# Mixture-of-experts stage: routed experts on their own tokens only, rows moved into expert order by indirect transfers

## The reference, cut to what matters

```python
logits = ((x @ wt.T) + repeat(g @ wg.T, s)) / 2        # 8 experts, g is per batch
scores = softmax(logits)
topk_w, topk_idx = top_k(scores, 2); topk_w /= topk_w.sum(-1) + 1e-20
gp = leaky(einsum('th,ehm->etm', x, w_gate)); up = einsum('th,ehm->etm', x, w_up)   # m = 128
y_all = einsum('etm,emh->eth', gp * up, w_down)
y = sum of the two chosen y_all, each by its weight
p = leaky(x @ sw_gate) * (x @ sw_up) @ sw_down         # shared expert, 256 wide
y = y + p
```

## Time and profile before

| what | us |
|---|---|
| median of 3 runs (lowest, highest) | 1475.9 (1474.04, 1478.81) |
| profiled execution: its time | 1475.61 |
| profiled execution: span, first to last instruction | 1473.6 |
| TensorE busy in the span | 1290.3 |
| VectorE busy | 1039.8 |
| ScalarE busy | 767.6 |
| GpSimd busy | 553.1 |
| next phase's first transfer is issued at | 440.37 |

### The profile page before, as it was taken

How to read it: one execution, slowest core, us unless ns; L and a number is a source line. 1 busy time by engine, 2 the same in 40 slices (tenths; PEclk the granted TensorE clock), 3 DMA queues, 4 the chain that set the end, 5 groups by cost and what they waited for, 6 DMA issues and landing times. The chain is left out here.

```text
span 1473.6 us, 30046 instructions
## 1 busy us (share of the span) xinstructions
PE 1290.3 (88%) x8705; PEld 996.1 (68%) x8710; DVE 1039.8 (71%) x2788; ACT 767.6 (52%) x1940; POOL 553.1 (38%) x834
## 2 busy tenths in 40 slices
PE   4989989998964799999999999999999999944866
PEld 2867877787842577777777777777777788731223
DVE  5566666656554777787877778868877877763986
ACT  3222223232221566666766766666767676624853
POOL 1333332333322675444444344444444444510004
PEclk9999999999986799999999999999999999976987
DMA  6232211220205300001000000010010000202115
GB/s 227 70 118 101 72 57 71 100 83 15 74 31 177 100 16 2 2 2 30 2 30 4 2 30 2 2 32 2 1 30 2 16 2 2 74 15 61 57 57 172
DMA packets 51043, 71.55 MB, mean 49 GB/s; under 512 B 4497, under 2 KB 43665, under 8 KB 48850
## 3 DMA queue, kind: packets, MB, share of 16 engines
q1 hardware_dynamic: 50338, 69.60, 14.3%
q10 hardware_dynamic: 560, 0.20, 0.1%
HBM read 57.07 MB, written 12.72 MB: 47 GB/s over the span
## 5 line engine op out<-in xcount | busy, mean ns | idle before, releaser
L837 POOL TENSOR_SCALAR scores<-scores,att_rinv 128x128 f32<-128x128 f32 (+3 forms) x512 | 264.3, 532 | 204.4 <-DVE att_rinv L1049 204.4
L893 ACT ACTIVATE scores<-scores,att_top 128x128 f32<-128x128 f32 (+3 forms) x512 | 281.5, 553 | 89.2 <-DVE att_top L1031 88.9
L1031 DVE CUSTOM_DVE_ANT_0 scores<-ps_y,w_bias_b,null_s 128x128 f32<-128x128 f32 x448 | 229.4, 547 | 100.5 <-PE ps_y L1181 89.1
L261 POOL TENSOR_TENSOR act_w<-act_g,wide_w 128x512 f32<-128x512 f32 x64 | 105.5, 1649 | 282.9 <-DVE act_g L379 277.4
L1192 PE MATMUL ps_up<-ident,scores 128*128 128x128 f32 x1280 | 191.7, 274 | 8.2 <-DVE keep L1059 6.2
L1180 PE MATMUL ps_y<-k_hh,q_hl 128*128 128x256 f32 (+2 forms) x512 | 187.6, 376 | 12.8 <-DVE att_top L1031 5.9
L1202 PE MATMUL ps_a<-keep,w_val 128*64 128x128 f32 x2560 | 197.2, 284 | 0.3 <-DVE keep L1059 0.3
L901 ACT ACTIVATE keep<-ps_up 128x128 f32<-128x128 f32 (+3 forms) x256 | 111.9, 437 | 156.1 <-PE ps_up L1192 153.2
L208 ACT ACTIVATE hid_hi<-hid 128x512 fp32r<-128x512 f32 x80 | 50.5, 631 | 241.8 <-DVE hid L397 241.7
L1192 PEld LDWEIGHTS ps_up<-ident,scores 128*128 128x128 f32 x1280 | 150.3, 140 | 30.9 <-issue 10.4
L844 POOL TENSOR_SCALAR w_q_hm<-q_hl 64x512 fp32r<-64x512 f32 x128 | 76.7, 612 | 239.0 <-ACT q_hl L916 239.0
(11 more groups left out here) (236 smaller groups left out, 2594.6 us busy)
## 6 DMA issues: line engine op xcount, KB each, us to landing
wide_w<-token_w_dram SPq DMA_DIRECT2D x16, 1024.0 KB, 4.7
x_raw<-in_x_t_dram SPq DMA_DIRECT2D x8, 512.0 KB, 3.7
x_nat<-in_x_nat_dram SPq DMA_DIRECT2D x8, 512.0 KB, 4.7
x_dram<-x_nat SPq DMA_DIRECT2D x8, 512.0 KB, 2.9
w_x1t<-x_dram SPq DMA_DIRECT2D x8, 512.0 KB, 4.0
c_dram<-out_raw SPq DMA_DIRECT2D x8, 512.0 KB, 3.2
c2t<-c_dram SPq DMA_DIRECT2D x8, 512.0 KB, 3.7
x_tile<-x_dram SPq DMA_DIRECT2D x8, 512.0 KB, 4.4
```

The source lines that it names most:

```text
L261: nc.gpsimd.tensor_tensor(act_w[:, k % 2], act_g[:, k % 2], wide_w[:, k], ALU.mult).then_inc(sem.act_w_ready, 1)
L837: nc.gpsimd.tensor_scalar(s, s, rinv[:, pp, q, hh:hh + 1], 0.0, ALU.mult, ALU.add).then_inc(sem.p_normed, 1)
L893: nc.scalar.activation(s, s, ACT.Exp, scale=-1.0, bias=top[:, pp, q, hh:hh + 1], accum_out=lsum[:, pp, q, hh:hh + 1]).then_inc(sem.exp_don ...
L1031: dve.tensor_tensor_reduce(scores_of(pp, hh, q), psS[:, hh, 0:n], bias_of(w, h)[:, CAUSAL[q]:CAUSAL[q] + n], 1.0, null_s[:, par, q, h:h + ...
```

## The change

The routed experts now work on the tokens that chose them. The batches are taken in two halves of 4 batches, 2048 tokens, 16 tiles of 128 tokens (HT = 16). In a half each token has two rows in a list in memory (`dram.xs`), ordered by expert, each expert's part filled up with rows of zeros to whole tiles of 128. The most tiles that can be needed is XT = 16 x 2 + 7 = 39, and the program always runs 39 a half, in JOBS = 20 steps of two tiles (the last has one); STEPS_X = 40.

The order of the work:

- Router: all of x is loaded first (`early_x`, 8 transfers of 512 KB). TensorE makes all logits as float32 products, tokens in the partitions, three for each of the 32 tiles of 128 tokens, the third of them adding the batch's condition.
- Routing, once for all tokens: VectorE finds both chosen experts (`pick`), TensorE counts with two products against a triangle and a matrix of ones (`ranks`, `counts`), VectorE works out each row's slot (`places_of`), the slots of the zero rows (`pads_of`) and each tile's expert (`owners_of`).
- GpSimd scatters x into `dram.xs`: one indirect transfer for each tile of tokens and choice, 32 a half, and 7 of zeros.
- The 16 shared units run as before, with their result copied to `p_all` by ScalarE. GpSimd's `weigh` is gone.
- Routed steps, pipelined over four stages: load two tiles (SyncE), transpose them, split hi and lo, gate and up with the tokens stationary and the expert's weights (256 columns, gate beside up) moving, leak, product, transpose, split, down, copy to `ys`, store to `dram.ys` (issued by ScalarE). TensorE reads each tile's expert into a register (`owner_of`) and uses it in the address of the weights.
- GpSimd gathers for each batch the 8 sets of 128 rows that its tokens need, and VectorE adds them to `p_all` with their weights (`combine`). The quantised product is as before, with its two casts on ScalarE (`widen`) in place of VectorE. Three batches do this beside routed steps (`DONE_AT`), the other five after them.

All of it is written out without loops. The mask of a head now waits for the bias of its pair of heads (`bias_in[h // 2]`).

```diff
-                def weigh(b, k):
-                    s = NE * b + k
-                    pool.wait_ge(sem.wide_in[2 * k // E], 16 * (b + 1))
-                    pool.wait_ge(sem.act_g_ready, s + 1)
-                    nc.gpsimd.tensor_tensor(act_w[:, k % 2], act_g[:, k % 2], wide_w[:, k], ALU.mult
-                                            ).then_inc(sem.act_w_ready, 1)
...
+                def scatter(h):
+                    pool.wait_ge(sem.nat_in[h], 16 * HB)
+                    pool.wait_ge(sem.routed, SLOTTED)
+                    for t in range(h * HT, (h + 1) * HT):
+                        for a in range(TOPK):
+                            nc.gpsimd.indirect_dma_start(
+                                dram.xs[h], bass.IndirectOffsetOnAxis(ap=slot[:, a, t:t + 1].bitcast(U32), axis=0),
+                                x_nat[:, t], None).then_inc(sem.scattered[h], 16)
+                    pool.wait_ge(sem.routed, PADDED)
+                    for n in range(PADS):
+                        nc.gpsimd.indirect_dma_start(
+                            dram.xs[h], bass.IndirectOffsetOnAxis(ap=pad_slot[:, h, n:n + 1].bitcast(U32), axis=0),
+                            zero[:], None).then_inc(sem.scattered[h], 16)
...
+                def gather(b):
+                    h = b // HB
+                    if b % HB == 0:
+                        for r in range(3):
+                            pool.wait_ge(sem.ys_out[h][r], stores(h, r))
+                    if b >= 2:
+                        pool.wait_ge(sem.combined, b - 1)
+                    elif b == 0:
+                        pool.wait_ge(sem.shared_done, UNITS_S)
+                        pool.wait_ge(sem.hl_ready, UNITS_S)
+                    for t in range(TT):
+                        for a in range(TOPK):
+                            nc.gpsimd.indirect_dma_start(
+                                got[b % 2][:, a, t], None, dram.ys[h],
+                                bass.IndirectOffsetOnAxis(ap=slot[:, a, b * TT + t:b * TT + t + 1].bitcast(U32), axis=0)
+                            ).then_inc(sem.gathered[b % 2], 16)
...
+                scatter(0)
+                scatter(1)
+                for k in range(EARLY):
+                    mask_diagonal(pool, nc, w, k, sem)
+                pool.wait_ge(sem.small_in, 3 * 16)
+                add_bias(0)
+                for b in range(HB):
+                    gather(b)
+                add_bias(1)
+                for b in range(HB, B):
+                    gather(b)
...
+                def owner_of(J, i):
+                    return pe.value_load(owner[0:1, J // JOBS, J % JOBS * 2 + i:J % JOBS * 2 + i + 1], min_val=0, max_val=E - 1)
...
+                    for i, e in enumerate(owners):
+                        for c in range(HC):
+                            last = three_products(pe, ps_g[J % 2][:, i], xt_hi[J % 2][:, c, i], xt_lo[J % 2][:, c, i],
+                                                  gu_hi[:, c, bass.ds(e, 1)].squeeze(1), gu_lo[:, c, bass.ds(e, 1)].squeeze(1),
+                                                  c == 0, c == HC - 1)
...
+                for s in range(LAST_STEP):
+                    if 0 <= s - 1 < STEPS_X:
+                        owners[s - 1] = [owner_of(s - 1, i) for i in range(tiles_of(s - 1))]
+                    if s < STEPS_X:
+                        turn_tiles(s)
+                    if 0 <= s - 1 < STEPS_X:
+                        tile_gate_up(s - 1, owners[s - 1])
+                    if 0 <= s - 2 < STEPS_X:
+                        turn_hidden(s - 2)
+                    if 0 <= s - 3 < STEPS_X:
+                        tile_down(s - 3, owners.pop(s - 3))
```

ScalarE and VectorE follow the same steps:

```diff
+                for s in range(LAST_STEP):
+                    if s < STEPS_X:
+                        turned_hi(s)
+                    if 0 <= s - 1 < STEPS_X:
+                        tile_leak(s - 1)
+                    if 0 <= s - 2 < STEPS_X:
+                        tile_hidden_hi(s - 2)
+                    if 0 <= s - 4 < STEPS_X:
+                        store_tiles(s - 4)
+                    if 0 <= s - 3 < STEPS_X:
+                        tile_out(s - 3)
...
+                for s in range(LAST_STEP):
+                    if s < STEPS_X:
+                        turned_lo(s)
+                    if 0 <= s - 1 < STEPS_X:
+                        tile_leaky(s - 1)
+                    if 0 <= s - 2 < STEPS_X:
+                        tile_hidden_lo(s - 2)
+                    if 0 <= s - 1 < STEPS_X:
+                        tile_hidden(s - 1)
+                    for b, at in enumerate(DONE_AT):
+                        if s == at:
+                            combine(b)
```

More of the change, by code:

```diff
@@ L70, in moe_phase @@
         router_g = sb("router_g", [G, E])
[L71 to L98, removed]
+        earlier = sb("earlier", [P, P], BF16)
+        every = sb("every", [P, P], BF16)
+        first = sb("first", [P, E])
+        pad_no = sb("pad_no", [P, PADS])
+        tile_no = sb("tile_no", [1, JOBS * 2])
+        slot = sb("slot", [P, TOPK, NT], I32)
+        pad_slot = sb("pad_slot", [P, HALVES, PADS], I32)
+        owner = sb("owner", [1, HALVES, JOBS * 2], I32)
+        weight = sb("weight", [P, TOPK, NT])
         amax = sb("amax", [P, TT])
@@ L160, in _ @@
+                for b in range(2, B):
+                    load_x(b)
                 load_projections(sp, dram, w, sem)
                 load_bias(sp, dram, w, range(EARLY), sem)
[L162 to L168, removed]
@@ L204, in hidden_hi @@
[L204 to L211, removed]
-                        s = NE * b + k
[L213 to L217, removed]
-                        if ahead and k == 3:
-                            exps(b + 1)
-                        if behind and k == 4:
-                            quantised_out(b - 1)
-                        if ahead and k == 6:
-                            weights_out(b + 1)
-                        hidden_hi(s, k % 2)
@@ new lines, in _ @@
+                nc.scalar.activation(rt[:, 1], rt[:, 0], ACT.Exp, scale=0.5).then_inc(sem.routed, 1)
+                split_hi(0)
+                for s in range(UNITS_S):
+                    b, k = s // SHARED, s % SHARED
+                    if k == 0 and b + 1 < B:
+                        split_hi(b + 1)
+                    leak_part(s)
+                    if s == 2:
+                        weight_hi(GU, 0)
+                    if s == 3:
+                        weight_hi(GU, 1)
+                    if s == 4:
+                        weight_hi(DN)
+                    if k == 1 and b >= 1:
+                        shared_out(b - 1)
+                    hidden_hi(s)
@@ L444, in _, with residual_wide @@
-                batch(B - 1, 1, False, True, False)
-                hidden_lo(NE * B - 1, 1)
-                quantise(B - 1, 1)
-                residual(B - 1, 1, 0)
-                residual(B - 1, 1, 1)
+                def residual_wide(b):
+                    for half in range(2):
+                        residual(b, half, z_wide[b % 2][:, 2 * half:2 * half + 2])
+                weight_lo(SG, 1)
+                weight_lo(SU, 2)
+                weight_lo(SD, 3)
+                route()
@@ new lines, in _ @@
+                pe.wait_ge(sem.routed, CHOSEN)
+                pe.matmul(ranks, earlier[:], chosen[:], start=True, stop=True)
+                pe.matmul(counts, every[:], chosen[:], start=True, stop=True).then_inc(sem.routed, 1)
+                gate_up(0)
+                gate_up(1)
+                for s in range(UNITS_S):
+                    if s + 2 < UNITS_S:
+                        gate_up(s + 2)
+                    down(s)
+                pe.wait_ge(sem.routed, OWNED)
+                pe.wait_ge(sem.routed, RANKS_READ)
```

936 lines of the change are left out of this document (593 added, 343 removed).

## The result

The changed kernel takes 1503.9 us (median of 4, 1502.0 to 1507.8) against 1477.4 for the kernel before: ratio 1.0185, 95% interval 1.0155 to 1.0214. It is 1.6 to 2.1% slower, where 1404 us was forecast, 5% faster. The profiled execution has a span of 1501.8 us, 28.2 more than before. The next phase's first transfer is issued at 471.5 us, where it was at 440.4, so the loss of 31 us and the missing gain all lie in the expert stage.

A forecast was written before the change was run, and what follows sets the result against it. TensorE was taken to bound the expert stage; routing to 57 us, shared units to 121, routed tiles to 302 and tail to 368.7 instead of 440.4 save 71.7 us: 1475.6 - 71.7 = 1404 us, range 1335 to 1470.

The forecast's parts named there:

- Step 1: Router and routing: logits at 35 us, slots at 52, the shared units' first VectorE instruction at 57.
- 48 x 0.213 = 10: Router: half of 96 fp32 products, which cannot start before the last x, at 0.213 us each, take 10 us.
- Steps 2 and 3: Shared units run to 121 us; the first half's scatters, done at 103, hide under them; the second ends by 154.
- c: GpSimd's time for one indirect transfer (scatter or gather), taken as 1.3 us.
- Step 4: Routed tiles, 126 to 302 us: first load 5 us, then 43 steps of 4.1 us, set by TensorE.
- 2.76 + 0.4: Routed step: 24 TensorE instructions at 0.115 us, plus four waiting groups at 0.1 us each to start.
- rival A: Routed steps and transfers: register loads run ahead, step 3.2 us, c = 1.0; 1355 us; chance 0.20.
- Step 5: Tail after the routed tiles, 302 to 369 us: 32 gathers take 41.6 us, then 21.7 until the next phase.
- B: Indirect transfers: each waits once for a VectorE instruction that holds GpSimd off, c = 2.0; 1435 us; chance 0.10.
- C: Scatters and gathers: GpSimd holds for each transfer's whole 2.9 us and becomes the bound; 1521 us; chance 0.12.
- D: Routed steps: gaps between groups lower TensorE's clock to about 0.50, step 6.4 us; 1503 us; chance 0.08.

The follow-up runs named there:

- Run 4: Against the changed kernel, router's 8-column weights made stationary with 512 tokens moving, logits transposed back; 1481.5 us, ratio 1.0040 to the kernel before.
- experiment 1: Against the changed kernel, GpSimd clears two small tiles and waits behind each of 142 indirect transfers; 1422.9 us, ratio 0.9642 to the kernel before.

## Why the prediction was wrong, by its steps

The removed work is gone: TensorE's busy time fell from 1290 to 1191 us. What failed is what took its place. The next phase was forecast at 368.7 us and measured at 471.5, 102.8 later, made up of the following.

**Step 1, router: wrong by 32 us.** Logits forecast at 35, measured 67.1. The term "48 x 0.213 = 10" had the price of one instruction (0.245 us measured) but half the count, and it assumed that the other half of the products would be done while x was still landing. They did not start before 19.9 us, so all 192 stood on the path, 47 us (19.9 to 67.1) at 1.00 of full clock. Run 4 gave 22.4 us back. The routing behind it was near: slots 86.8 - 67.1 = 19.7 us after the logits against 17; the first VectorE instruction of the shared units at 91.1 against 57 (+34).

**Steps 2 and 3, "hidden": wrong by 70 us.** The price of a scatter was right: c = 1.27 us alone, where I took 1.3, and 1.48 in the mean of the first half (57.6/39); the first half ended at 144.5 against 103, the second at 194.0 against 154. Of the 41.5 and 40 us of delay 34.8 came from the later slots, the rest from VectorE beside the scatters. The cover was what failed: I took the scatters to cost the shared units nothing, with no row behind it. The shared units took 134 us from 91.1 to 225.0 against 64, and with spacing 72. So some 62 us of the 70 are the held-up issue; the other 8 were not taken apart (the granted clock from 88 to 130 us is 0.92 in the spaced run, where I had priced full clock). I had asked whether GpSimd would be done in time and whether VectorE would slow it, never whether its transfers would slow the engines beside them.

**Step 4: the size wrong on the good side, then eaten.** First tile load 3.0 us against 5. Undisturbed, 442 matrix instructions in 60 us are 18.4 steps, 3.26 us each instead of 4.1. My own 2.76 + 0.4 leaves 0.1 for both register loads, where I had 0.9: they cost little, as rival A had it (3.2). In the spaced run the steps take 138 us where I said 176. But the hold-ups beside the gathers made it 166.4 (228.0 to 394.4): 10 us less than forecast in place of 38.

**Step 5, tail: 77.1 us against 66.7.** 394.4 to 471.5. The last hold-up (412.9 to 447 us) lies in it, and the second bias addition (385.1 to 394.4) stands ahead of its first gather; their shares were not measured apart.

34.1 (first VectorE instruction of the shared units) + 69.9 (shared units) - 2 (first load) - 9.6 (steps) + 10.4 (tail) = 102.8 us. The sign was lost by the hold-up: without it (experiment 1), and with the router as it was, the kernel is 3.6% faster than before, and with the router mended too it reaches 1387.5, below the forecast of 1404.

**Rivals.** A was right on the step; c was 1.27, as forecast, and not its 1.0. B was right in mechanism and small in effect (1.48 in the mean of the first half, not 2.0): beside VectorE instructions with two SBUF inputs a scatter took up to 3.03 us instead of 0.96 (111.88 us in the timeline above). The Trainium skill's rule (SBUF — State Buffer, SBUF: two separate sides), that GpSimd cannot write descriptors while VectorE holds the shared ports, agrees with these rows. By theory S it even protected the kernel here: as long as VectorE slowed GpSimd to 1.54 us a scatter, nothing piled up. C gave the sign and nearly the size (1521), but for a reason that is not there: GpSimd does not hold for a transfer's 2.9 us. D gave 1503, the right number by a wrong way, which is luck: the granted clock is 1.00 in the undisturbed steps, and where it is near 0.50 (140 to 200 us, 400 us on) TensorE had stood idle before (busy for 0.6 of the 20 us from 140 to 160). The Trainium skill (DMA: Bandwidth & Descriptors, Anatomy of one DMA — SWDGE (gpsimd) path) puts little of a GpSimd transfer into making descriptors; for plain transfers 0.54 us each fits, for indirect ones it does not, since 0.96 of each 1.27 us is GpSimd's own instruction, and there the measurement decides.

## What to carry to other kernels

Work on an idle engine is free only if it disturbs nobody: where the profile of before has no instance of an operation, price what it does to its neighbours as well as what it takes. When engines idle for "issue" inside a group that has no waits, look for what all of them share and what runs at a steady beat beside them; a kernel that gets faster by adding idle work to one engine has found it. And before a small product is called cheap, count its instructions and the columns of weights each of them loads: the operand with 8 columns belongs on the stationary side.

## What the hardware showed that I had not expected

- Indirect transfers from GpSimd, back to back at 1.27 us, hold up the issue of TensorE, VectorE and ScalarE (single products 2.80 us apart). At 1.61 us they don't, at 1.46 they still do (26 of the 81 us that spacing brings are missing). The hold-up ends about 1.46 us times the number of transfers after the first one of a burst began, 4 to 8 us behind the last one. It began 50 us into the first burst, which VectorE had slowed, some 7 us after it went at 1.27 undisturbed, and also some 7 us into the first gathers' burst.
- While it lasts, the start times of single products on TensorE are near multiples of 0.70 us apart (1.40, 2.10, 2.80, 3.50, within 0.05).
- Half the rows change the price of a transfer from 1.46 to 1.39 us; plain transfers of the same size from the same engine, at 0.54 us each, hold nobody up.
- A stream of 600 products without a wait, begun before the stretch, went through at 0.12 us each; the same stream with waits that were already met took 136 us.
- What the engines share with the indirect transfers stays open.
